# Feed-forward of a linear-attention and local-attention block: the 85-wide third chunk in column groups of 64 and 32, computed first

## The reference, cut to what matters

```
h = shift_token(x)                      # second half of the channels from the token before
h = (h - mean) / sqrt(var + 1e-5) * lg + lb
h = h @ w1 + b1                         # 128 -> 2 * 341
a, g = split(h, 2)
x = x + (a * gelu(g)) @ w2 + b2         # 341 -> 128
```

## Time and profile before

| | |
|---|---|
| median of 3 runs | 1754.42 us (1753.64 to 1755.47) |
| the profiled execution, own time | 1755.7 us |
| its span, first to last instruction | 1753.9 us |
| mean granted TensorE clock | 0.991 |
| busy PE, PEld | 1674.9 us (95%), 1154.1 us (66%) |
| busy DVE, ACT, POOL | 1446.5 (82%), 1299.2 (74%), 1039.0 us (59%) |
| phase F of layer 0, first and last start of the down-projection | 934.34 to 1053.38 us, then one behind the seam at 1064.61 |
| phase F of layer 1, the same | 1617.06 to 1741.86 us |

### The profile page before, as it was taken

The page is one execution under the profiler, slowest core; times in us unless marked ns, Lnnn a source line. Parts: engine busy times, 40 slices in busy tenths (PEclk is TensorE's granted clock), DMA queues, the critical chain, the costliest instruction groups (busy, mean ns, idle before and its releaser), DMA issues. The chain is left out here.

```text
span 1753.9 us, 54573 instructions
## 1 busy us (share of the span) xinstructions
PE 1674.9 (95%) x18245; PEld 1154.1 (66%) x18373; DVE 1446.5 (82%) x3283; ACT 1299.2 (74%) x3588; POOL 1039.0 (59%) x1015
## 2 busy tenths in 40 slices
PE   6999999979999999999989997999999999998997
PEld 4666666646777777777765664777777777775664
DVE  3777777769999999999967776899999999986996
ACT  5888888848998998989982224998998998985221
POOL 1333333337777777777763324777777777775664
PEclk9999999989999999999999999999999999999999
DMA  3211111111111111111113321111111111113443
GB/s 118 69 48 48 48 48 48 43 43 35 44 39 39 42 40 37 42 42 36 42 50 94 92 76 37 38 43 45 33 42 45 33 42 45 33 40 88 110 122 86
DMA packets 201095, 94.02 MB, mean 54 GB/s; under 512 B 82578, under 2 KB 192060, under 8 KB 201020
## 3 DMA queue, kind: packets, MB, share of 16 engines
q1 hardware_dynamic: 201020, 93.06, 20.1%
HBM read 51.00 MB, written 25.23 MB: 43 GB/s over the span
## 5 line engine op out<-in xcount | busy, mean ns | idle before, releaser
L846 ACT ACTIVATE pr<-banks,nb,rr 128x128 f32<-128x128 f32 x1024 | 456.3, 465 | 5.0 <-DVE nb L915 5.0
L747 POOL TENSOR_TENSOR rr<-ss,half_neg 128x16 f32<-128x16 f32 x128 | 374.4, 2925 | 19.0 <-POOL ss L744 17.0
L764 POOL TENSOR_TENSOR pr<-pr,rl 128x512 f32<-128x512 f32 x256 | 266.5, 1041 | 103.3 <-DVE rl L877 103.3
L885 DVE TENSOR_REDUCE ss<-sq 128x16 f32<-128x1024 f32 x128 | 156.1, 1219 | 75.4 <-ACT sq L795 61.3
L846 ACT ACTIVATION_READ_ACCUMULATOR pr<-banks,nb,rr 128x1 f32 x1024 | 216.5, 211 | 0.0
L1216 ACT ACTIVATE f_g<-banks,b_s 128x512 f32<-128x512 f32 (+1 forms) x96 | 65.9, 686 | 202.0 <-PE banks L1300 192.2
L893 DVE TENSOR_REDUCE mx<-banks 128x8 f32<-128x1024 f32 x128 | 156.0, 1219 | 9.0 <-PE banks L1022 8.3
L383 POOL TENSOR_SCALAR a_ve<-a_mv 128x2 f32<-128x2 f32 x96 | 21.4, 223 | 226.5 <-DVE a_mv L394 223.4
L755 POOL TENSOR_TENSOR krot<-ka,rr 128x512 f32<-128x512 f32 x128 | 134.4, 1050 | 22.3 <-POOL rr L747 11.7
L974 PE MATMUL banks<-ident,pr 128*128 128x128 f32 x1024 | 141.2, 281 | 5.9 <-POOL pr L764 5.9
L837 ACT COPY pT<-banks 128x512 f32<-128x512 f32 x128 | 75.1, 587 | 95.9 <-PE banks L974 95.9
(11 more groups left out here) (126 smaller groups left out, 4210.4 us busy)
## 6 DMA issues: line engine op xcount, KB each, us to landing
ve<-vt SPq DMA_DIRECT2D x128, 128.0 KB, 2.2
hs<-y_d SPq DMA_DIRECT2D x128, 64.0 KB, 2.0
yt<-y_d SPq DMA_DIRECT2D x64, 128.0 KB, 2.1
y_d<-yn SPq DMA_DIRECT2D x64, 128.0 KB, 2.0
f_h<-y_d SPq DMA_DIRECT2D x128, 64.0 KB, 2.0
f_y<-y_d SPq DMA_DIRECT2D x64, 128.0 KB, 2.2
xa<-in_L_attn_x SPq DMA_DIRECT2D x32, 128.0 KB, 2.2
xr<-in_L_attn_x SPq DMA_DIRECT2D x32, 128.0 KB, 2.3
```

Source lines behind the costliest of these rows:

```text
L747: nc.gpsimd.tensor_tensor(rr[:, r, :], ss[:, r, :], half_neg[:], ALU.pow).then_inc(T["rr"], 1)
L764: nc.gpsimd.tensor_tensor(pr[:, e], pr[:, e], rl[:, e].unsqueeze(2).broadcast_to([P, UH, P]), ALU.mult).then_inc(T[("ne", "no")[e]], 1)
L846: a = nc.scalar.activation(pr[:, e, j, :], bank[e][:, j * P:(j + 1) * P], ACT.Exp, bias=nb[:, X.t, UH * e + j:UH * e + j + 1], scale=rr[:, ...
L885: nc.vector.tensor_reduce(ss[:, 2 * X.p + X.t, :], sq[:].rearrange("p (h d) -> p h d", d=DH), AX.X, ALU.add).then_inc(T["ss"], 1)
```

## The change

The third chunk is cut again, in 64 and 21 columns. For the 64 columns the 512 tokens are taken as two halves of 256 that are computed side by side in PSUM partitions 0 to 63 and 64 to 127, columns 0 to 255 of the bank. For the last 21, 32 columns of w1 are taken (11 of them a second time, so that the group is 32 wide), and the four tiles of 128 tokens are computed side by side in partitions 0, 32, 64, 96, columns 256 to 383. Gelu and gate become two instructions each, of 256 and 128 columns on 128 partitions, and write a new tile `f_ut`. Since the down-projection wants these rows from partition 0 up, six transfers on SP in each step (`f_tail`) copy them from `f_ut` into `f_u`, and `f_pe_down` waits for them. The order of chunks is now 2, 0, 1. The bias of the third chunk is loaded in twelve transfers in place of two for each layer.

```diff
+    LAST = (HC - 1) * P
+    TAIL, OLD = HID - 32, 32 - (HW[-1] - 64)
...
+        b1_t = sb("b1_t", [P, L, 2, 2])
...
-                    for g in range(2):
+                    for g in range(2 if c < HC - 1 else 0):
...
+                for g in range(2):
+                    for rows, first, k in ((64, LAST, 0), (32, TAIL, 1)):
+                        for r in range(0, P, rows):
+                            with nc.allow_non_contiguous_dma(reason="a bias, once"):
+                                load_late(sp, b1_t[r:r + rows, l, g, k:k + 1],
...
+        f_ut = sb("f_ut", [P, 2, 3 * P])
...
+        ORDER = (2, 0, 1)
...
+        def f_tail(sp, l, i, odd=False):
+
+            p = par_of(i, odd)
+            m = l * M + i
+            sp.wait_ge(G["u"], HC * m + ORDER.index(HC - 1) + 1)
+            if not isinstance(m, int):
+                apart(sp)
+            until(sp, G["w_ps"], m - 1)
+            if not isinstance(m, int):
+                apart(sp)
+            for h in range(2):
+                sp.dma_start(f_u[0:64, p, HC - 1, 256 * h:256 * h + 256], f_ut[64 * h:64 * h + 64, p, 0:256]
+                             ).then_inc(G[f"ut{p}"], 16)
+            for t in range(FT):
+                sp.dma_start(f_u[64:HW[-1], p, HC - 1, t * P:(t + 1) * P], f_ut[32 * t + OLD:32 * t + 32, p, 256:384]
+                             ).then_inc(G[f"ut{p}"], 16)
...
+                    nc.scalar.activation(f_g[:, c, 0:256], bank[2 + q % 2][:, 0:256], ACT.Gelu, bias=b1_t[:, l, 1, 0:1])
+                    nc.scalar.activation(f_g[:, c, 256:384], bank[2 + q % 2][:, 256:384], ACT.Gelu,
+                                         bias=b1_t[:, l, 1, 1:2]).then_inc(G["g"], 1)
...
+                    nc.vector.scalar_tensor_tensor(out=f_ut[:, p, 0:256], in0=bank[A_BANK[q]][:, 0:256],
...
+                    nc.vector.scalar_tensor_tensor(out=f_ut[:, p, 256:384], in0=bank[A_BANK[q]][:, 256:384],
...
+            def up(c, into, first):
+                if c < HC - 1:
+                    return nc.tensor.matmul(into[:], w1_s[:, l, first + c * P:first + c * P + P], f_hT[:, p, :],
+                                            start=True, stop=True)
+                for h in range(2):
+                    nc.tensor.matmul(into[64 * h:64 * h + 64, 0:256], w1_s[:, l, first + LAST:first + LAST + 64],
+                                     f_hT[:, p, 256 * h:256 * h + 256], start=True, stop=True)
+                for t in range(FT):
+                    j = nc.tensor.matmul(into[32 * t:32 * t + 32, 256:384], w1_s[:, l, first + TAIL:first + HID],
+                                         f_hT[:, p, t * P:(t + 1) * P], start=True, stop=True)
+                return j
+
+            for q in chunks:
+                k = HC * m + q
+
+                until(pe, G["g"], k - 1 if q else k)
+                up(ORDER[q], bank[2 + q % 2], HID).then_inc(G["g_ps"], 1)
                 until(pe, G["u"], k - HC + 1)
...
+                up(ORDER[q], bank[A_BANK[q]], 0).then_inc(G["a_ps"], 1)
...
         def f_pe_down(pe, l, i, odd=False):
             pe.wait_ge(G["u"], HC * (m + 1))
+            pe.wait_ge(G[f"ut{p}"], 96 * (M // 2 * l) + 96 * half_count(i))
...
-                return ((lambda i, **k: f_sync(sp, l, i, **k), 3), (lambda i, **k: f_sync_y(sp, l, i, **k), 2),
+                return ((lambda i, **k: f_tail(sp, l, i, **k), 0), (lambda i, **k: f_sync(sp, l, i, **k), 3), (lambda i, **k: f_sync_y(sp, l, i, **k), 2),
                         (lambda i, **k: f_store(sp, l, i, **k), -1))
```

More of the change, by code:

```diff
@@ L89, in build @@
     HW = [min(P, HID - c * P) for c in range(HC)]
+    LAST = (HC - 1) * P
+    assert 64 < HW[-1] <= 96
+    TAIL, OLD = HID - 32, 32 - (HW[-1] - 64)
     tabs_np = rotary_tables(N)
@@ L196, in late_loads @@
                                       b1[l, g * HID + c * P:g * HID + c * P + HW[c]].rearrange("(p a) -> p a", a=1))
+                for g in range(2):
[3 more added lines that the diff above has]
+                                load_late(sp, b1_t[r:r + rows, l, g, k:k + 1],
+                                          b1[l, g * HID + first:g * HID + first + rows].rearrange("(p a) -> p a", a=1))
             else:
@@ L363, in build @@
         G = {k: sem("F_" + k) for k in (
-            "in0", "in1", "y_in0", "y_in1", "x1_in0", "x1_in1", "st", "mv", "ve", "rs", "xn", "hT_ps", "hT", "g_ps", "a_ps", "g", "u", "yb", "w_ps", "yn",
+            "in0", "in1", "y_in0", "y_in1", "x1_in0", "x1_in1", "st", "mv", "ve", "rs", "xn", "hT_ps", "hT", "g_ps", "a_ps", "g", "u", "ut0", "ut1", "yb", "w_ps", "yn",
             "st2", "mv2", "ve2", "rs2", "ln", "o", "out0", "out1")}
@@ L1211, in f_act @@
             m = l * M + i
[L1212 to L1217, removed]
+            for q in range(HC):
+                c = ORDER[q]
+                act.wait_ge(G["g_ps"], HC * m + q + 1)
+                until(act, G["u"], HC * (m - 1) + q + 1)
+                if c < HC - 1:
+                    nc.scalar.activation(f_g[:, c, :], bank[2 + q % 2][:], ACT.Gelu,
+                                         bias=b1_s[:, l, 1, c:c + 1]).then_inc(G["g"], 1)
+                else:
+                    nc.scalar.activation(f_g[:, c, 0:256], bank[2 + q % 2][:, 0:256], ACT.Gelu, bias=b1_t[:, l, 1, 0:1])
+                    nc.scalar.activation(f_g[:, c, 256:384], bank[2 + q % 2][:, 256:384], ACT.Gelu,
+                                         bias=b1_t[:, l, 1, 1:2]).then_inc(G["g"], 1)
         def f_dve_stats(dve, l, i, odd=False):
@@ L1248, in f_dve_gate @@
             until(dve, G["w_ps"], m - 1)
[L1249 to L1255, removed]
+            for q in chunks:
+                c = ORDER[q]
+                dve.wait_ge(G["g"], HC * m + q + 1)
+                dve.wait_ge(G["a_ps"], HC * m + q + 1)
+                if c < HC - 1:
+                    nc.vector.scalar_tensor_tensor(out=f_u[:, p, c, :], in0=bank[A_BANK[q]][:],
+                                                   scalar=b1_s[:, l, 0, c:c + 1], in1=f_g[:, c, :],
+                                                   op0=ALU.add, op1=ALU.mult).then_inc(G["u"], 1)
+                else:
+                    nc.vector.scalar_tensor_tensor(out=f_ut[:, p, 0:256], in0=bank[A_BANK[q]][:, 0:256],
+                                                   scalar=b1_t[:, l, 0, 0:1], in1=f_g[:, c, 0:256],
+                                                   op0=ALU.add, op1=ALU.mult)
+                    nc.vector.scalar_tensor_tensor(out=f_ut[:, p, 256:384], in0=bank[A_BANK[q]][:, 256:384],
+                                                   scalar=b1_t[:, l, 0, 1:2], in1=f_g[:, c, 256:384],
+                                                   op0=ALU.add, op1=ALU.mult).then_inc(G["u"], 1)
         def f_dve_out(dve, l, i, odd=False):
@@ L1294, in f_pe_up @@
             pe.wait_ge(G["hT"], m + 1)
[L1295 to L1301, removed]
+            def up(c, into, first):
+                if c < HC - 1:
+                    return nc.tensor.matmul(into[:], w1_s[:, l, first + c * P:first + c * P + P], f_hT[:, p, :],
[7 more added lines that the diff above has]
+                return j
+            for q in chunks:
+                k = HC * m + q
+                until(pe, G["g"], k - 1 if q else k)
+                up(ORDER[q], bank[2 + q % 2], HID).then_inc(G["g_ps"], 1)
                 until(pe, G["u"], k - HC + 1)
-                if isinstance(i, int) and i == 0 and c == 1:
+                if isinstance(i, int) and i == 0 and q == 1:
                     pe.wait_ge(T["yn"], 2 * B * (l + 1))
-                nc.tensor.matmul(bank[A_BANK[c]][0:w, :], w1_s[:, l, c * P:c * P + w], f_hT[:, p, :],
-                                 start=True, stop=True).then_inc(G["a_ps"], 1)
+                up(ORDER[q], bank[A_BANK[q]], 0).then_inc(G["a_ps"], 1)
         def f_pe_down(pe, l, i, odd=False):
```

## The result

The changed kernel takes 1802.59 us (median of 4, 1801.59 to 1808.15) against 1754.95 before: ratio 1.028, interval 1.0267 to 1.0292. It is 47.6 us slower. The forecast was slower by 13.3 us, 1767.7, with a range up to 1776. The profiled execution took 1808.15 us for a span of 1806.4, 52.5 us more span than before, so its parts add up to somewhat more than the medians differ. Of these 52.5 us, 2.3 lie ahead of the first down-projection of layer 0, 13.4 between its first and its last, 2.2 between the two layers, 33.0 between the first and the last of layer 1, and 1.5 behind that.

What follows compares the result with a forecast made beforehand. PE was taken to bound the kernel, with SP becoming the bound in layer 1. Layer 0 2.2 us, layer 1 10.4 and bias loads 0.7 summed to 13.3 us more, 1767.7 us; range 1759 to 1776.

Steps and rivals of the forecast that it cites:

- What bounds it: Phase F: PE sets the pace at 8.50 us a step; SP has 2.3 us free in layer 1, 3.5 in layer 0.
- Part 1: Third chunk's narrow matmuls in phase F: width changes outweigh saved columns, 0.14 us more a step (bounds -0.15 to +0.4).
- Rival B: Narrow passes cost only their columns, but SP fills in layer 1: 1758.6 us; chance 0.06.
- Part 2: Third chunk's split gelu and gate on ACT and DVE: nothing to 0.1 us more each, hidden.
- Part 3: Six f_tail transfers on SP: 2.9 us a step (bounds 2.4 and 3.4), making layer 1 9.15 us a step.
- it fits: Layer 0: SP busy 5.0 + 2.9 = 7.9 us of a step of 8.64, so only the matmuls' loss remains.
- Rival D: SP fills in both layers, 0.56 us an issue, tail 3.7 us: 1778 us; chance 0.09.
- A: SP does not fill, small issues cost 0.2 us or less, tail 1.6 us: 1760 us; chance 0.12.
- C: Packing pays its full 0.43 us a step, tail stays below 2.0 us: about 1746 us; chance 0.05.
- The chain in layer 1: From tail through landed rows, f_h, statistics and store to the tail two steps on: 18.3 us, 9.15 a step.
- The end: Layer 1's last tail stands behind a store and f_x, so the last down-projection comes 2.5 us later.
- Part 4: Ten more bias-load issues per layer on SP in phase A: 0.7 us for both layers together.

Runs made afterwards that it cites:

- matmuls alone: Changed kernel without its six transfers, the down-projection reading the third chunk's rows from f_ut: 1760.06 us against 1755.04, ratio 1.0031.
- the grouped passes: Changed kernel without transfers, both products' 64-wide passes first, then both 32-wide ones, three width changes a step, not five: 1753.67 us, ratio 0.9994.

## Why the prediction was wrong

The direction was right, and so was the mechanism in layer 1; the size was not, and layer 0 was taken to stay at PE's pace. One term of the sum carries both misses.

- **What bounds it.** Right for layer 1: PE set the pace before, and SP does now, which the forecast found from its 2.3 us of free time. Wrong for layer 0, which the forecast left to PE; SP sets the pace there too.
- **Part 1, the matmuls.** Right. Forecast 0.14 us a step, 4.5 us in all; matmuls alone measured 5.0 us. The two products took 1.88 us against 1.86 worked out from the earlier trace rows. The step grew by 0.18 and not 0.14. The timelines of PE without transfers show where: the narrow part took 0.16 us more than the full-width chunk, 0.02 over the forecast, and the way into it 0.10 and 0.16 us in turn, against 0.08 and 0.15 for the wait before. Rival B, where the narrow passes cost their columns alone, falls with the run of the matmuls alone and with the grouped passes.
- **Part 2.** Right: busy times of ACT and DVE moved by less than 1 us in thirteen steps.
- **Part 3, the six transfers. This step failed**, in its price of an issue. It took 0.44 us for a transfer of 21 rows and an upper bound of "0.51 like any other". Measured, to the next start, were 0.78, and 0.60 for the 64-row ones: the tail was 4.65 us a step and not 2.9, outside the bounds of 2.4 and 3.4. The sum also slipped: its 2.65 us is 6 x 0.44, though it had put the two 64-row issues at 0.51, which would have made 2.8; that is a small part of the 1.75 us missed. The nearest rows had been read too kindly in two ways. The 64-row row comes from issues that stand alone; the first of our two costs 0.47 to 0.54 us, but one right behind another from SBUF to SBUF 0.59. And the lower price of the 85-row bias loads was carried over to 21 rows, as if fewer rows were cheaper; those loads come from DRAM, in rows of 4 bytes. The same six transfers beside the old matmuls gave all but the whole loss. With 4.65 in the forecast's own sums SP is busy 5.0 + 4.65 = 9.7 us in layer 0 and 6.2 + 4.65 = 10.9 in layer 1, which are the measured steps to 0.1 us. Layer 0, "it fits", then does not: that is 12.9 us in place of 1.8 for thirteen steps, and layer 1 29.2 in place of some 8.
- **Rival D** (SP fills in both layers) was the right case, at a chance of 0.09 and with 0.56 us an issue still too cheap: it gave 1778. A and C, the cheap issues, fall.
- **The chain in layer 1.** Its parts were there: DVE waits for `f_h` (28.1 us) more than PE for the copied rows. (It puts the way from the statistics to the store at 9.0 us where it had read 9.1, which is of no weight.) With the tail at 4.65, SP's own sum is the tighter bound, and the steps follow it.
- **The end.** 2.5 us forecast; the last gap between down-projections grew by 3.3 us, and from there to the end it is 13.5 us in place of 12.0, all of it the slower passes of the last down-projection (4.46 us in place of 2.94, at a granted clock of 0.64), which no term of the forecast had.
- **Part 4, the bias loads.** Forecast 0.7 us; the traces show none. From the first narrow block of phase A to the last, with all but two of these loads behind the first block's start, PE takes 338.86 us in both kernels (29.43 to 368.29 us before, 30.11 to 368.96 after). The first down-projection of layer 0 does start 2.3 us later (936.6 against 934.34 us), but 0.7 us of that lie ahead of the first block, where the other runs with these loads differ by 1.2 us among themselves, and 1.6 between the last one and the first transfer of phase T. In the runs with the same loads it started between 931 and 936 us, so such a shift comes and goes without them. The 2.2 us between the layers are as little explained: in the other runs that stretch is 552.4 to 556.7 us long, against 552.4 before.

The miss of part 3 was one of range as much as of value. An operation absent from the trace had been given an upper bound equal to the dearest row of its kind, though none of these rows had both of its properties (SBUF to SBUF in a row, a count of rows not divisible by 16).

## What to carry to other kernels

Count the issues of a transfer queue as an engine of its own, with its busy time per step, before adding to it: two more were free here, six cost 43 us, and which of the two holds depends only on the free time that a view of busy engines does not show. Narrow matmuls side by side save columns (0.43 us a step here), but each change of the column groups' width takes about 0.15 us with the weights that follow, so a split must save more than its changes cost, and passes of one width belong together. If rows must be copied inside SBUF, copy a multiple of 16, even if some of them are not wanted (15 us here).

## What the runs showed of the hardware

An issue on SP from SBUF to SBUF, right behind another such, costs 0.59 us with 16, 32 or 64 rows (8, 16 and 64 KB), 0.71 with 21 and 0.75 with 24; a transfer between SBUF and DRAM of twice the size costs one issue (0.40 us). The Trainium skill has a rule that bears on the counts. "DMA: Bandwidth & Descriptors", section "Why a DMA increments its semaphore by 16 and not by 1", says that a transfer runs on the largest number of engines up to 16 that divides its rows, and that the issuing sequencer itself writes what is then missing of the semaphore's 16. Our 21 and 24 rows are such cases and pay 0.12 to 0.16 us more, which fits; that the write is what costs, no run here shows. The bias loads of 85 rows, 273 ns at least and 331 at most, are such a case too and were cheap, while most of the changed kernel's loads of 32 and 64 rows of the same bias took 0.41 to 0.60 us. So the rule alone does not price an issue, and for such loads a multiple of 16 was not the cheap one.

PE's granted clock was lower behind some of the waits for the copied rows. Busy time by stretch of the changed kernel, a wait of PE in layer 1, the down-projection behind it, and the last one:

```profile
1707.30:1709.10 1.80, 0.00 (x0) 0.00 (x0) 1.80 (x7) 0.00 (x0) 0.57 (x1) 1.00 0.05 12
1709.16:1713.10 3.94, 3.94 (x25) 3.94 (x26) 1.38 (x7) 0.00 (x0) 0.64 (x1) 0.70 0.50 121
...
1792.80:1797.30 4.50, 4.46 (x24) 4.26 (x24) 0.00 (x0) 0.00 (x0) 0.07 (x1) 0.64 0.23 62
```

Behind an idle stretch of 1.8 us the granted clock averaged 0.70, a mix of the 1.2 and the 2.4 GHz level, and the 24 passes took 4.11 us in place of 2.84; other waits of the same length left it at full (at 1698.27 us the passes took 2.94). In the last down-projection, behind 4.5 us idle, it averaged 0.64 and the passes took 4.46 us. In between this cost nothing that shows: the step of 1709.16 us is 10.9 us like its neighbours, since SP sets the pace. At the end it cost 1.5 us.
